# Causal masks added by VectorE's fused add and minimum, in place of mask products on TensorE

## The reference, cut to what matters

```python
xn = _layernorm(x, ln_w)                                 # 8 x 178 x 192
Q = xn[:, None, :, :] * W_qk[None, :, None, :]           # 12 heads; queries are the keys
attn = jnp.einsum('bhse,bhte->bhst', Q, Q) / math.sqrt(eb)
attn = jnp.where(causal[None, None], attn, -jnp.inf)
attn = jax.nn.softmax(attn, axis=-1)
out = jnp.einsum('bhst,bhte->bhse', attn, xn[:, None, :, :] - avg_wte)
out = out * N_reg[None, None, :, None]                   # then @ W_o.T, residual, experts
```

## Time and profile before

| | us |
|---|---|
| median of 3 runs | 456.36 (456.19 to 456.52) |
| the profiled execution | 454.25 |
| span of its instructions | 452.4 |
| TensorE busy | 441.1 |
| VectorE busy | 271.6 |
| ScalarE busy | 182.4 |
| GpSimd busy | 67.7 |

### The profile page before, as it was taken

One profiled execution on the slowest core, in us unless ns is written; L12 is line 12 of the kernel. 1 busy time (PEld: TensorE's weight loads), 2 busy tenths in 40 slices (PEclk: granted clock), 3 DMA queues, 4 the chain that ended last, 5 costly groups with the idle time before them and its releaser, 6 DMA issues.

```text
span 452.4 us, 7150 instructions
## 1 busy us (share of the span) xinstructions
PE 441.1 (97%) x2666; PEld 384.8 (85%) x2666; DVE 271.6 (60%) x725; ACT 182.4 (40%) x565; POOL 67.7 (15%) x92
## 2 busy tenths in 40 slices
PE   8699999999999999999998999999999999999996
PEld 7487779977799776898777999999999999999995
DVE  4478956277572896626869655578653475433433
ACT  1476568244692356823541144553213412112111
POOL 3013221132122312210002313322002000000000
PEclk9699999999999999999999999999999999999999
DMA  7967999999999999997350034221221221323210
GB/s 208 270 257 134 211 212 212 213 213 213 214 213 213 213 213 214 212 213 206 118 193 2 0 121 154 60 74 45 90 80 66 68 66 40 105 67 77 64 43 35
DMA packets 20997, 63.62 MB, mean 141 GB/s; under 512 B 2572, under 2 KB 10836, under 8 KB 20578
## 3 DMA queue, kind: packets, MB, share of 16 engines
q0 software_dynamic: 7552, 39.39, 41.3%
q1 hardware_dynamic: 12546, 22.78, 17.3%
q10 hardware_dynamic: 864, 1.00, 0.7%
HBM read 61.88 MB, written 1.27 MB: 140 GB/s over the span
## 4 chain that ended last, share of the span: by engine, by line
PE 93%; DVE 3%; DMA 1%; ACT 1%; issue 1%; POOL 0%; SPq 0%; DVEq 0%; POOLq 0%
PE bank L810 15%; PE bank L927 15%; PE bank L759 7%; PE bank L696 5%; PE bank L897 5%; PE bank L898 5%; PE bank L895 5%; PE bank L896 5%; PE bank L894 5%; PE bank L750 4%; PE bank L707 3%; PE bank L698 3%; PE bank L724 2%; PE bank L760 2%; PE bank L711 2%; PE bank L660 1%
## 5 line engine op out<-in xcount | busy, mean ns | idle before, releaser
L810 PE MATMUL bank<-woT,area_o 128*128 128x192 f32 (+1 forms) x432 | 72.3, 327 | 0.0
L810 PEld LDWEIGHTS bank<-woT,area_o 128*128 128x128 f32 (+1 forms) x432 | 69.8, 182 | 0.6 <-issue 0.6
L517 ACT ACTIVATE pm<-bank,nmax 128x128 f32<-128x128 f32 x96 | 34.5, 369 | 81.3 <-DVE nmax L1028 81.3
L1124 DVE TENSOR_TENSOR area_b<-area_b,area_w 128x484 f32<-128x484 f32 (+1 forms) x36 | 24.1, 668 | 51.7 <-ACT area_b L590 50.4
L432 POOL DMA_DIRECT2D area_w<-in_L_attn_wte_dram x26 | 31.1, 1215 | 128.4 <-DMA area_w<-in_L_attn_wte_dram 128.4
L590 ACT ACTIVATE area_b<-bank,area_k 128x484 f32<-128x484 f32 (+1 forms) x24 | 15.8, 657 | 59.7 <-PE bank L898 59.7
L759 PE MATMUL bank<-pT,xn 128*128 128x356 f32 x96 | 39.7, 495 | 0.0
L540 ACT ACTIVATE area_b<-xb,w 64x192 f32<-64x192 f32 x96 | 38.3, 447 | 0.8
L894 PE MATMUL bank<-area_w_r,area_o_r 128*128 128x484 f32 (+1 forms) x84 | 37.3, 444 | 0.0
L927 PE MATMUL bank<-area_k,area_b 128*128 128x192 f32 (+1 forms) x192 | 35.3, 326 | 0.0
L927 PEld LDWEIGHTS bank<-area_k,area_b 128*128 128x128 f32 (+1 forms) x192 | 31.6, 182 | 0.9
(11 more groups left out here) (217 smaller groups left out, 932.5 us busy)
## 6 DMA issues: line engine op xcount, KB each, us to landing
area_w<-in_L_attn_wte_dram POOLq DMA_DIRECT2D x28, 1344.0 KB, 12.6
area_w<-gate_rows SPq DMA_DIRECT2D x24, 242.0 KB, 3.2
area_k<-in_experts_dram SPq DMA_DIRECT2D x8, 353.0 KB, 5.3
area_w<-gate_rows SPq DMA_DIRECT2D x12, 228.0 KB, 3.2
area_a<-in_experts_dram SPq DMA_DIRECT2D x6, 353.0 KB, 5.4
area_b<-gate_rows SPq DMA_DIRECT2D x8, 242.0 KB, 3.0
woT<-in_L_attn_W_o_dram SPq DMA_DIRECT2D x1, 1728.0 KB, 14.8
area_o<-in_x_dram SPq DMA_DIRECT2D x4, 384.0 KB, 8.3
```

Of the source, the lines that this page charges most:

```text
L517: act.activation(pm[:, sl, n, :], SIDE[k][:, j * P:(j + 1) * P], ACT.Exp, bias=nmax[:, sl, n:n + 1], accum_out=psums[:, sl, n:n + 1])
L810: last = pe.matmul(o, oT[:, c, at:at + n], woT[:, c, :], start=(c == 0), stop=(c == NCH - 1))
```

## The change

The mask products go, and with them identb. cmask and tmask become f32; tmask gets 128 columns of zeros ahead of its triangle, so that it covers all 178 columns of a tail. VectorE's maxima become six tensor_tensor_reduce instructions a unit in place of four reductions: each reads scores from PSUM and a mask from SBUF, writes -(score + mask) to pm or pt in SBUF and the minimum of that, which is minus the maximum, to nmax. The exponentials read pm and pt and write them in place, with scale -1. The scores of a unit wait for max_of of the unit before, no longer for exp_of. VectorE's maxima wait for turned_tail of two units before, as they now write the half of pm and pt that it read.

```diff
-        identb = sb("identb", [P, P], BF16)
-        cmask = sb("cmask", [P, P], BF16)
-        tmask = sb("tmask", [P, 64], BF16)
+        cmask = sb("cmask", [P, P])
+        tmask = sb("tmask", [P, P + 64])
...
-            own.mark(pool.affine_select(out=tmask[0:64, :], in_=tmask[0:64, :], compare_op=ALU.is_ge, fill=MASKED,
+            own.mark(pool.affine_select(out=tmask[0:64, P:P + 64], in_=tmask[0:64, P:P + 64], compare_op=ALU.is_ge, fill=MASKED,
...
-            own.mark(pool.tensor_copy(identb[:], ident[:]))
...
-                        act.activation(pm[:, sl, n, :], SIDE[k][:, j * P:(j + 1) * P], ACT.Exp,
+                        act.activation(pm[:, sl, n, :], pm[:, sl, n, :], ACT.Exp, scale=-1.0,
                                        bias=nmax[:, sl, n:n + 1], accum_out=psums[:, sl, n:n + 1])
-                    act.activation(pt[:, sl, k, :], SIDE_TAIL[k], ACT.Exp, bias=nmax[:, sl, 4 + k:5 + k],
+                    act.activation(pt[:, sl, k, :], pt[:, sl, k, :], ACT.Exp, scale=-1.0, bias=nmax[:, sl, 4 + k:5 + k],
...
                     if U:
-                        pe.wait_ge(exp_of[k], U)
+                        pe.wait_ge(max_of[k], U)
...
-                for k in range(2):
-                    pe.matmul(mains[k], identb[:], cmask[:].rearrange("p (a t) -> p a t", a=1).broadcast_to([P, 2, P]),
-                              start=False, stop=False, skip_group_check=True)
-                    pe.matmul(SIDE_TAIL[k][:, P:S], identb[:], tmask[:, 0:TAIL], start=False, stop=False,
-                              skip_group_check=True)
...
                 sl = u % 2
+                if U >= 2:
+                    dve.wait_ge(turned_tail, U - 1)
                 for k in range(2):
                     dve.wait_ge(scores_of[k], U + 1)
-                    dve.tensor_reduce(nmax[:, sl, 2 * k:2 * k + 2], SIDE[k].rearrange("p (j t) -> p j t", j=2), AX.X,
-                                      ALU.max, negate=True)
-                    dve.tensor_reduce(nmax[:, sl, GRP + k:GRP + k + 1], SIDE_TAIL[k], AX.X, ALU.max,
-                                      negate=True).then_inc(max_of[k], 1)
+                    for j in range(2):
+                        n = 2 * k + j
+                        dve.tensor_tensor_reduce(out=pm[:, sl, n, :], in0=SIDE[k][:, j * P:(j + 1) * P], in1=cmask[:], scale=-1.0,
+                                                 scalar=-NEVER, op0=ALU.add, op1=ALU.min, accum_out=nmax[:, sl, n:n + 1])
+                    dve.tensor_tensor_reduce(out=pt[:, sl, k, :], in0=SIDE_TAIL[k], in1=tmask[:, 0:S], scale=-1.0,
+                                             scalar=-NEVER, op0=ALU.add, op1=ALU.min,
+                                             accum_out=nmax[:, sl, GRP + k:GRP + k + 1]).then_inc(max_of[k], 1)
```

More of the change, by code:

```diff
@@ L392, in _ @@
             pool.wait_ge(pool_own, own.at)
-            own.mark(pool.affine_select(out=tmask[64:P, :], in_=tmask[64:P, :], compare_op=ALU.is_ge, fill=MASKED,
+            own.mark(pool.affine_select(out=tmask[64:P, P:P + 64], in_=tmask[64:P, P:P + 64], compare_op=ALU.is_ge, fill=MASKED,
                                         base=0, pattern=[[-1, 64]], channel_multiplier=1))
@@ L689, in scores @@
                 h = GRP * g
-                mains = [m.rearrange("p (j t) -> p j t", j=2) for m in SIDE]
                 splits = [m.rearrange("p (j c t) -> p j c t", j=2, c=2) for m in SIDE]
```

## The result

The changed kernel takes **450.4 us** (median of 4 runs, 448.01 to 452.11), the kernel before on the same chip 456.27 us (455.46 to 456.52): a ratio of 0.9871, 95% interval 0.9823 to 0.9918. That is 5.9 us less, where 6.8 were forecast. Two more sets of runs gave 0.9889 (0.9863 to 0.9916) and 0.9864 (0.9844 to 0.9884).

What follows compares the result with a forecast made beforehand. TensorE's own instruction stream was taken as the bound (93% of the span). 6.65 + 0.2 - 0.1 = 6.75, say 6.8 us saved, gave 449.6 us; range 448.5 to 452.0, own range 448.9 to 450.4 (chance 0.62).

Steps and rivals of the forecast that it cites:

- rival 1: Table stream moves up less or not at all; VectorE waits 2.1 us, TensorE 0.4 to 1: 450.3 to 451.5, chance 0.16.
- The masks' products, 6.65 us: TensorE's stream without mask products: 0.27 us saved in each of 23 units, 0.44 in the first; bounds 6.0 and 8.9.
- rival 5: TensorE's change from 128 to 64 rows costs nothing behind L698, so more is saved: 447.3 us, chance 0.05.
- rival 4: No change: the removed products filled time in which TensorE would have waited anyway: 456.4 us, chance 0.03.
- The changed wait, 0.2 us: TensorE's next scores wait for maxima, not exponentials: 0.2 us gained in the second unit, nothing more in steady units.
- VectorE, 0.7 us more a unit: VectorE's six fused instructions replace four reductions; accumulator reads priced at 0.09 us each as on ScalarE; 0.7 us more taken.
- the low end: VectorE's extra work if accumulator reads are not separate instructions: 0.2 us more a unit.
- rival 2: VectorE's fused op runs at half rate, 1.7 us more a unit, some 5 us back to TensorE: 454.5 us, chance 0.09.
- VectorE's cover: VectorE's lead of 2.1 to 2.3 us, restored in long units, hides its extra work; TensorE sees nothing of it.
- rival 3: VectorE becomes the bound: break-even at 1.8 us more a unit; at 0.6 us per instruction 463 us; chance 0.05.
- ScalarE, "nothing": ScalarE's six exponentials a unit read SBUF instead of PSUM; 3 us of room a unit, so no cost.
- The table stream: Table transfers on GpSimd's queue end near 208.1 us; VectorE waits 1.2 us for the table sum; 0.1 us charged.

Runs made afterwards that it cites:

- the kernel with products kept: Changed kernel with four zero products of the masks' shape put back in TensorE's stream each unit: 454.36 us, ratio 0.9966.
- the doubled instructions: Changed kernel with each of VectorE's six fused instructions a unit issued twice, first into spare buffers: 462.85 us, ratio 1.0149.
- the wide mean: The table mean's one-column products made 128 or 64 columns wide: 448.72 us on the changed kernel, 455.32 on the one before, 448.63 with GpSimd's power also earlier.
- the doubled one: Changed kernel with the one-column products of the table's mean issued twice: 454.28 us.

## Why the prediction was right, and where it was off

The measured change is -5.9 us (450.4), the forecast -6.8 (449.6); the time lies in the range, where the forecast's own range ends (450.4) and rival 1's begins (450.3). The mechanism came as forecast: the masks' stretch is the gain, and VectorE's taking them over costs TensorE nearly nothing. That the sum also came so close is in part luck, since terms missed on both sides cancel.

- **The masks' products, 6.65 us.** Right. 0.25 us from L695's second start to L699, 6.01 for 6.28, and the same 6.01 in the kernel that only leaves them out. The change of rows keeps its 0.10 us behind L695, so rival 5 falls; rival 4 too. In the first unit the step gave 0.51 us, not 0.44: "everything taking twice as long" holds for L695 (0.30 us), and the change of rows took 0.13 at the lower clock, not 0.20. The unit as a whole does not show it: the half-clock stretch ends at 23.16 for 22.09 while the scores start only 0.44 later, so more of the unit lies in it (6.94 for 6.99).
- **The changed wait, 0.2 us.** Too low, by two causes. In the second unit it gives 0.37 by the kernel with products kept, 0.48 by the old wait put back. And the step "In steady units scores never waited for it, so nothing more there" is wrong twice. In the old units the wait took 0.1 us in two of them (6.39 and 11.88 us, 6.28 and 11.78 with products kept). In the shorter ones it would bind wherever VectorE is late: 0.2 to 0.5 us in four units with the old wait put back, 0.8 in one with the masks left out. The new wait avoids that; at equal clock it is worth about 1.1 us, of few executions.
- **VectorE, 0.7 us more a unit.** Off, and the low end was right: 0.2. The step was to take ScalarE's 0.09 us per accumulator read over to VectorE. The Trainium skill ("VectorE: DVE Perf Modes", section "Two Vector instructions with no wait between them") counts an op that writes out its accumulator as two instructions. The trace agrees on the number of rows, and shows that here the second costs no step (0.21 us from start to start for 128 columns, of which 0.13 are the columns at 1.04 ns). No halved rate either: rival 2 falls. What that rival quotes of two sources in SBUF no run here tests.
- **VectorE's cover.** The work is hidden, as said. The point from which it is not was set too far: rival 3 gave back 6.9 us at 1.8 us more a unit than before, and the doubled instructions, 0.2 + 1.4 = 1.6 us more than before, lost 12.4 us. The sum of rival 3 does not follow from its own terms either: 12 units that fall behind by 1.6 to 1.8 us each, less 4 x 2.3 us of lead, are 10 to 12 us. Beside it, the long unit at the end of a pair grew too (14.36 us), which the step had as giving time back.
- **ScalarE, "nothing".** Nearly right. Its exponentials take 0.26 us more a unit. In the sixth unit of the first pair TensorE, which now comes earlier, waits 0.56 us for ScalarE's copy of the turned probabilities (L524), a wait that the kernel before does not have; the unit lasts 11.77 us, and 11.88 less 0.27 is 11.61. So at least 0.16 us are lost there, of which the exponentials' share was not separated.
- **The table stream.** Right in kind. GpSimd's restart came at 35.30, 35.81 and 34.89 in the changed kernel's three profiles, for 35.54, and the stream's end at 208.67, 208.72 and 208.34, for 209.02. The start of an execution moves these times; counted from the second unit's start the restart stands at 10.0 us in all three and at 10.64 before, so the step from VectorE's statistics to the restart is as said, and gave 0.64 us. In the profile shown first VectorE came late itself; in the other two the forecast wait is there, 0.5 and 1.0 us for 1.2, and costs nothing and 0.26 for 0.1. Rival 1's wait of 2.1 us is in none. What was missed is that the same stream stands ahead of GpSimd's powers: the step that GpSimd "has 0% of the chain" and so "Nothing" counted its work and not its place in line.
- **The clock.** No term of the sum, and what moves single executions most. 10 of 14 executions of the changed kernel have the lower mean clock, 27 of 54 of the kernel before, at 1.9 and 1.3 us each; 10/14 x 1.9 - 1/2 x 1.3 = 0.7 us would be most of the 0.9 that the forecast was off. These shares are too few to say so: it is an account that fits, not one that is shown. What is shown is that the clock falls behind the mean's one-column products, by the wide mean (0 of 20) and the doubled one (10 of 10); when it does and when not stays open.

## What to carry to other kernels

When one engine's stream gets shorter, look at every pace that does not get shorter with it. A request in a queue behind such a stream is safe by a number of microseconds, and that number shrinks by what the change gains: from 3.0 us to 0.2 or none here, after which one place in the queue was worth 7.3 us. And where steps of 1 to 2 us appear between executions of one kernel, read the granted clock stretch by stretch before looking for a wait, and compare profiles from a point behind the start, which alone differs by 0.9 us between profiles of one kernel here.

## What the runs showed of the hardware that was not expected

- A fused add-and-minimum of VectorE with one source in PSUM, a full result and an accumulator goes at the price of a plain tensor_tensor: 0.21 us for 128 columns and 0.26 for 178. ScalarE's accumulator read holds the next activation back by 0.09 us, VectorE's holds it back by none.
- The granted clock fell to 0.50 for 3.41 us while TensorE was busy without a gap, 0.9 us after a run of one-column products; in none of 20 executions with the same sums 128 and 64 columns wide is the mean clock below 0.991. Not every run of one-column products is followed by such a fall: 27 of 54 executions of the kernel before have the lower mean, and none of the eleven with the products kept.
- The change from products on 128 rows (L695) to products on 64 (L699) costs 0.10 us at a granted clock of 1.00 and 0.13 at 0.50.
- ScalarE's exponentials of 128 columns took 391 ns from SBUF and 369 from PSUM; from start to start the difference is larger, 0.39 us for 0.34.
